# Attention scores as plain fp32 matmuls on 32 rows in place of three fp32r products

## The chip, the cores and the metric

One core of one Trainium2 chip. The time is the device time of one execution in microseconds (us). Engines in the rows: PE is TensorE's matmuls, PEld its weight loads, DVE is VectorE, ACT is ScalarE, POOL is GpSimd, SP is SyncE.

## The reference

Two cross-attention layers in fp32 over 16 batches of 128 tokens (x is 16 x 128 x 256, the context 16 x 128 x 192), 16 heads of 16:

```python
def _L0_xattn_ref(x, y, ...):
    xn = layernorm(x, ln1_w, ln1_b); yn = layernorm(y, ln2_w, ln2_b)
    q = (xn @ Wq) ...; k, v = split(yn @ Wkv)            # 16 heads of 16
    attn = softmax(einsum('bhqd,bhkd->bhqk', q, k) * scale)
    x = x + (einsum('bhqk,bhkd->bhqd', attn, v) @ Wproj + bproj)
    h = gelu(layernorm(x, ln3_w, ln3_b) @ W1 + b1, approximate=False)
    return x + (h @ W2 + b2)

def _L1_xattn_ref(x, encoder_out, norm_w, wq, wkv, wout):
    xn = x * rsqrt(mean(x * x) + EPS_RMS) * norm_w
    q = xn @ wq; k, v = split(encoder_out @ wkv)
    q = rotate(q, cos, sin); k = rotate(k, cos, sin)
    q = q / maximum(norm(q), EPS_L2); k = k / maximum(norm(k), EPS_L2)
    attn = softmax(einsum('bqhd,bkhd->bhqk', q, k) * sqrt(HEAD_DIM))
    return x + einsum('bhqk,bkhd->bqhd', attn, v) @ wout
```

## The kernel before, in words

A tile is one batch: 128 tokens, which stand in the 128 partitions. Three stages follow one another. Stage A is the attention of the first layer, stage B its MLP (two tiles at a time), stage C the second layer. x stays on the chip in x_all from the first load to the last store. Each engine has its own program, with the order of its steps written out by hand: step_a(s) and step_c(p, j) name what an engine does in step s, for tiles s, s-1, s-2 and so on, and semaphores tie the engines together.

In stage A, TensorE's step_a(s) is: queries and keys of tile s-1 (L722, L726, plain fp32, into bank_qk, already transposed: 256 query rows and 256 key rows as four blocks of 128 x 128), the turn of the finished heads of tile s-5 (L820), values of tile s-2 (L736, plain fp32), scores_a of tile s-2, the weighted values of tile s-4 (L800, plain fp32, one matmul for each of 16 heads, into four column quadrants of 32), the output projection of tile s-5 (L828), the turn of the maxima of tile s-3 (L770), the turn of the inputs of tile s (L708, L710), the turn back of tile s-4 (L811), and shifted_a of tile s-3.

scores_a gives the scores with the queries down the partitions, from which VectorE takes each row's maximum (row_max, L1203, two instructions of 128 x 1024). shifted_a computes the same scores once more, the other way round, and subtracts the maxima by further matmuls (L782, fp32r), and ScalarE takes the exponentials of these (L477). Both call score_terms, which is one score call below.

A head has 16 rows, and a quadrant of 32 partitions holds two heads. So one side of the product is in `masked`: two copies of qkT, each multiplied by a column of halves_t (ones on the 16 rows of one head of each quadrant, zeros on the other), side by side as 256 columns. One matmul on 32 rows then gives both heads. Before the change each operand is split into a high part of type fp32r and a low part (what is left, fp32r too), and the product is the sum of three fp32r matmuls, (hi, hi), (hi, lo), (lo, hi), by HI_LO. In stage A ScalarE makes the high part (queries_keys_hi, L446) and both masked copies of it (L454); VectorE makes the low part (queries_keys_lo, L1193), and GpSimd both masked copies of that (L342). A ring of RING = 3 buffers holds them.

In stage C, TensorE's step_c is: back_c, queries and keys (L697, fp32r, three products), units_T (the turn of the unit vectors, L1021, into bank_o), values_c (L697), weighted_c (L834), inputs_c (L992, L994), project_c (L697), normed_c (the turn of `on`, L1062, into bank_o as well), scores (L1032). ScalarE's units_hi writes the masked high parts of the queries and the high part of the keys from bank_o (L631 twice, L633), VectorE's units_lo the low parts (L1389 twice, L1392). normed_c waits for units_lo, because it overwrites bank_o. GpSimd takes -0.5 powers (L413, 128 x 32) for the unit vectors.

VectorE's step_a(s) is: statistics(s), heads_a(s-5), residual_a(s-6), normalise(s), queries_keys_lo(s-1), maxima(s-2); its step_c has units_lo behind turns and turned, and ahead of square_sums and inputs_lo. Each engine goes through its list strictly in order.

Of the kernel before, what the change touches and what calls it, by code (L numbers as in the profile page):

```python
# [39 lines left out]
NG = 4  # L40
# [52 lines left out]
def build(nc, x, ctx, ln1_w, ln1_b, ln2_w, ln2_b, ln3_w, ln3_b, Wq, Wkv, Wproj, bproj, W1, b1, W2, b2,  # L93
          norm_w, wq, wkv, wout, rope, halves, picks, out):
    es = ExitStack()
    with es:
# [98 lines left out]
        def att_sems(n):  # L195
# [6 lines left out]
        a_centred, a_qk_hi, a_qk_lo, a_masked_hi, a_masked_lo = (  # L202
            sem(f"a_{k}") for k in ("centred", "qk_hi", "qk_lo", "masked_hi", "masked_lo"))
# [5 lines left out]
        c_rope, c_turned, c_rot, c_rot_sq, c_norm_sq, c_norm_min, c_norm_inv, c_unit, c_unit_hi, c_unit_lo = (  # L209
            sem(f"c_{k}") for k in ("rope", "turned", "rot", "rot_sq", "norm_sq", "norm_min", "norm_inv", "unit", "unit_hi", "unit_lo"))  # L210
# [94 lines left out]
        def _(pool):  # L305
# [28 lines left out]
            def masked_lo(t):  # L334

                if ok(t):
                    r = t % RING
                    pool.wait_ge(a_qk_lo, t + 1)
                    wait(pool, a_shifted, t - 2)
                    for half in range(2):  # L340
                        ones = halves_t[:, half:half + 1].unsqueeze(2).broadcast_to([128, 4, TOK])
                        nc.gpsimd.tensor_tensor(masked[:, r, 1, :, half, :], qkT_r[:, r, 1, :, :].bitcast(fp32), ones, ALU.mult)\  # L342
                            .then_inc(a_masked_lo, 1)

            def step_a(s):
                inverse_std(s)
                residual_bias(s)
                masked_lo(s - 1)
# [7 lines left out]
            masked_lo(0)  # L356
# [3 lines left out]
            masked_lo(1)  # L360
            residual_bias(3)
            masked_lo(2)
            inverse_std(4)
            residual_bias(4)
            masked_lo(3)
# [59 lines left out]
        def _(act):  # L425
# [15 lines left out]
            def queries_keys_hi(t):  # L441

                if ok(t):
                    act.wait_ge(A["qk_mm"], t + 1)
                    wait(act, a_shifted, t - 2)
                    nc.scalar.activation(qkT_r[:, t % RING, 0, :, :], bank_qk[:, :].rearrange("p (a b) -> p a b", a=4), ACT.Copy)\  # L446
                        .then_inc(a_qk_hi, 1)

            def masked_hi(t):

                if ok(t):
                    act.wait_ge(a_qk_hi, t + 1)
                    for half in range(2):
                        nc.scalar.activation(masked[:, t % RING, 0, :, half, :], qkT_r[:, t % RING, 0, :, :].bitcast(fp32),  # L454
                                             ACT.Copy, scale=halves_t[:, half:half + 1]).then_inc(a_masked_hi, 1)
# [51 lines left out]
            def step_a(s):  # L507
                exps_a(s - 4)
                queries_keys_hi(s - 1)
                on_T(s - 5)  # L510
                masked_hi(s - 1)
# [12 lines left out]
            queries_keys_hi(0)  # L524
            inputs_T(1)
            masked_hi(0)
            values_a(0)
            queries_keys_hi(1)
            inputs_T(2)
            masked_hi(1)  # L530
            values_a(1)
            queries_keys_hi(2)
            maxima_T(0, bank_y)
            inputs_T(3)
            masked_hi(2)
            exps_a(0)
            queries_keys_hi(3)
            masked_hi(3)
# [86 lines left out]
            def units_hi(t, j):  # L625

                if ok(t):
                    act.wait_ge(c_turned, t + 1)
                    wait(act, C["scores"], NG * (t - 1))
                    for half in range(2):  # L630
                        nc.scalar.activation(pair[:, j, 0, :, half, :], bank_o[:, 0:C1].rearrange("p (a b) -> p a b", a=KT),  # L631
                                             ACT.Copy, scale=halves_t[:, half:half + 1]).then_inc(c_unit_hi, 1)
                    nc.scalar.activation(qkT_r[:, j, 0, KT:, :], bank_o[:, C1:].rearrange("p (a b) -> p a b", a=KT), ACT.Copy)\  # L633
                        .then_inc(c_unit_hi, 1)
# [25 lines left out]
            def step_c(p, j):  # L660
# [4 lines left out]
                units_hi(s - 3, 1 - j)  # L665
# [25 lines left out]
        def _(pe):  # L691
# [21 lines left out]
            def queries_keys_a(t):  # L713

                if ok(t):
                    j = t % 2
                    pe.wait_ge(A["inT_ready"], t + 1)
                    wait(pe, a_qk_lo, t)
# [771 lines left out]
```

## Time and profile before

| | us |
|---|---|
| median of 3 runs | 385.97 |
| lowest and highest | 385.35, 391.71 |
| span of the profiled execution | 386.9 |

The profiled execution has no time of its own beside its span, which runs from its first to its last instruction; it stands 0.9 us above the median of the timed runs. Stage A runs to about 150 us of the span, stage B to about 265, stage C to the end. TensorE is busy 356.5 us (92%), VectorE 294.4, ScalarE 239.3, GpSimd 197.1. A busy share is an average over the span: what bounds a stage is read from the chain of waits in that stage. TensorE's records overlap, so the sum of their lengths is more than the time that they take.

### The profile page before, as it was taken

To read this page: it belongs to the slowest core of one execution; us is meant where nothing else is said; L and a number is where in the kernel's file an instruction comes from. 1 tells how busy PE (TensorE), PEld (TensorE's weight loads), DVE (VectorE), ACT (ScalarE), POOL (GpSimd) and SP (SyncE) were. 2 spreads that over 40 slices of the span, in tenths; PEclk is the share of its full clock that TensorE was granted. 3 is DMA by queue.
4 is the path that set the end of the run, shared out by engine and by line. 5 is a ranking of instruction groups with operands and counts; after the bars stand their busy time and mean duration, and the time that the engine had idled before them with its cause. 6 is when DMAs were issued, how large, how long until landed. Compare 5 with 4: busy or idle time off the path is not lost.

```text
span 386.9 us, 11499 instructions
## 1 busy us (share of the span) xinstructions
PE 356.5 (92%) x4475; PEld 318.7 (82%) x4475; DVE 294.4 (76%) x654; ACT 239.3 (62%) x464; POOL 197.1 (51%) x177
## 2 busy tenths in 40 slices
PE   8998999999999989898999999978889989989974
PEld 5977888888888867798999998978778878878854
DVE  4799987989899773267755559467899999999752
ACT  2356677666677655815644476163877777777862
POOL 2474544554665611003331233248899998999810
PEclk9999999999999999999999999999999999999999
DMA  6853001110000000000000000000001001010001
GB/s 157 246 158 121 27 25 43 32 28 25 2 3 4 22 2 2 2 2 0 0 0 0 0 0 3 10 22 0 22 12 36 26 26 42 29 37 14 29 30 41
DMA packets 14432, 12.39 MB, mean 32 GB/s; under 512 B 2996, under 2 KB 13752, under 8 KB 14392
## 3 DMA queue, kind: packets, MB, share of 16 engines
q1 hardware_dynamic: 14384, 11.83, 10.4%
q8 instruction: 28, 0.46, 0.5%
q14 instruction: 12, 0.10, 0.1%
q10 hardware_dynamic: 8, 0.00, 0.0%
HBM read 9.73 MB, written 2.10 MB: 31 GB/s over the span
## 4 chain that ended last, share of the span: by engine, by line
PE 58%; issue 22%; DVE 10%; ACT 5%; POOL 4%; POOLq 0%; DVEq 0%; ACTq 0%
PE bank_qk L697 9%; PE banks_s L745 6%; PE bank_y L834 4%; PE bank_y L828 3%; PE banks_s L1032 3%; PE bank_t L800 3%; PE bank_qk L722 3%; PE bank_o L736 3%; PE bank_t L697 3%; PE bank_qk L726 3%; DVE row_max L1203 2%; POOL x_all L375 2%; PE bank_y L1052 2%; PE bank_o L1021 2%; PE bank_y L929 1%
## 5 line engine op out<-in xcount | busy, mean ns | idle before, releaser
L413 POOL TENSOR_TENSOR norm_inv<-norm_sq_min,minus_half 128x32 f32<-128x32 f32 x16 | 87.5, 5468 | 1.8 <-DVE norm_sq_min L1374 1.8
L576 ACT ACTIVATE W_s<-banks_s,b_cols 128x256 f32<-128x256 f32 x60 | 25.0, 469 | 41.3 <-PE banks_s L915 41.3
L342 POOL TENSOR_TENSOR masked<-qkT_r,halves_t 128x512 fp32r<-128x512 f32 x32 | 32.9, 1050 | 24.1 <-DVE qkT_r L1193 24.1
L477 ACT ACTIVATE PT<-banks_s 128x1024 f32<-128x1024 f32 x32 | 31.0, 1022 | 20.3 <-PE banks_s L782 18.3
L1203 DVE TENSOR_REDUCE row_max<-banks_s 128x8 f32<-128x1024 f32 x32 | 37.6, 1218 | 7.7 <-PE banks_s L745 7.7
L368 POOL TENSOR_TENSOR b_var_eps<-b_mean_var,eps_t 128x2 f32<-128x2 f32 x8 | 1.6, 197 | 69.1 <-DVE b_mean_var L1137 69.1
L915 PE MATMUL banks_s<-lnT_hi,W_hi 128*128 128x256 f32 x120 | 34.2, 285 | 0.0
L915 PE MATMUL banks_s<-lnT_hi,W_lo 128*128 128x256 f32 x120 | 33.9, 283 | 0.0
L915 PE MATMUL banks_s<-lnT_lo,W_hi 128*128 128x256 f32 x120 | 33.9, 283 | 0.0
L642 ACT ACTIVATE PT<-banks_s 128x1024 f32<-128x1024 f32 x32 | 31.1, 1024 | 4.1 <-PE banks_s L1032 4.1
L745 PE MATMUL banks_s<-masked,qkT_r 32*128 32x256 f32 x768 | 31.5, 294 | 1.6 <-DVE row_max L1203 1.3
L745 PEld LDWEIGHTS banks_s<-masked,qkT_r 32*128 32x128 f32 x768 | 25.0, 184 | 9.5 <-issue 7.7
L1298 DVE TENSOR_TENSOR hT_lo<-W_s,hT_hi 128x512 fp32r<-128x512 f32 x32 | 24.6, 793 | 10.2 <-ACT hT_hi L580 10.1
L375 POOL TENSOR_TENSOR x_all<-x_all,b_row 128x256 f32 (+1 forms) x16 | 15.8, 1005 | 16.0 <-DVE qk_unit L1149 16.0
L915 PEld LDWEIGHTS banks_s<-lnT_hi,W_hi 128*128 128x128 f32 x120 | 23.0, 192 | 0.2 <-issue 0.2
L915 PEld LDWEIGHTS banks_s<-lnT_lo,W_hi 128*128 128x128 f32 x120 | 23.0, 192 | 0.0
L915 PEld LDWEIGHTS banks_s<-lnT_hi,W_lo 128*128 128x128 f32 x120 | 23.0, 192 | 0.0
L454 ACT ACTIVATE masked<-qkT_r,halves_t 128x512 fp32r<-128x512 f32 x32 | 21.3, 718 | 0.0
L929 PE MATMUL bank_o<-W_hi,hT_hi 128*128 128x256 f32 x64 | 19.1, 299 | 1.5 <-DVE hT_lo L1298 1.4
L580 ACT ACTIVATE hT_hi<-W_s 128x512 fp32r<-128x512 f32 x31 | 19.6, 632 | 1.0
L319 POOL TENSOR_TENSOR var_eps<-mean_var,eps_t 128x2 f32<-128x2 f32 x16 | 3.1, 196 | 33.5 <-DVE mean_var L1168 33.5
L834 PE MATMUL bank_y<-PT,vals 128*17 128x128 f32 x512 | 17.1, 274 | 2.6 <-ACT PT L642 2.6
(171 smaller groups left out, 1095.6 us busy)
## 6 DMA issues: line engine op xcount, KB each, us to landing
ctx_in<-in_ctx SPq DMA_DIRECT2D x32, 96.0 KB, 2.0
x_all<-in_x SPq DMA_DIRECT2D x16, 128.0 KB, 2.1
W_s<-in_L_xattn_W SPq DMA_DIRECT2D x2, 1024.0 KB, 6.4
out<-Wq_s SPq DMA_DIRECT2D x16, 128.0 KB, 1.8
Wq_s<-in_L_xattn_Wq SPq DMA_DIRECT2D x1, 256.0 KB, 3.0
Wkv_s<-in_L_xattn_Wkv SPq DMA_DIRECT2D x1, 256.0 KB, 3.2
Wproj_s<-in_L_xattn_Wproj SPq DMA_DIRECT2D x1, 256.0 KB, 4.2
wout_s<-in_L_xattn_wout SPq DMA_DIRECT2D x1, 256.0 KB, 3.0
```

The lines of the kernel that those rows point to most:

```text
L342: nc.gpsimd.tensor_tensor(masked[:, r, 1, :, half, :], qkT_r[:, r, 1, :, :].bitcast(fp32), ones, ALU.mult)\
L375: nc.gpsimd.tensor_tensor(tile_of(2 * p + j), tile_of(2 * p + j), b2_row[:, :], ALU.add).then_inc(b_bias, 1)
L413: nc.gpsimd.tensor_tensor(norm_inv[:, j, :], norm_sq_min[:, j, :], minus_half[:, :], ALU.pow)\
L477: nc.scalar.activation(PT[:, 2 * h:2 * h + 2, :], banks_s[:, 2 * h:2 * h + 2, :], ACT.Exp, scale=HD ** -0.5)\
L576: last = nc.scalar.activation(hT[:, m, :], (bank or bank_s[u])[:, 256 * k:256 * k + 256], ACT.Gelu, bias=b1_cols[:, m:m + 1])
L642: nc.scalar.activation(PT[:, 2 * h:2 * h + 2, :], banks_s[:, 2 * h:2 * h + 2, :], ACT.Exp, scale=HD ** 0.5)\
L697: last = mm(out, a[:, x, k, :], b[:, y, k, :], start=k == n == 0, stop=k == 1 and n == 2)
L745: last = mm(bank_s[g][:, 2 * TOK * tile:2 * TOK * (tile + 1)], qkT_r[quad(g), r, a, rows + tile, :], masked[quad(g), r, b, columns + tile, ...
L834: last = mm(out[32 * r:32 * r + VW, 128 * g:128 * g + 128], vals[:, j, GH * g + r, :], PT[:, g, 128 * r:128 * r + 128], start=True, stop=True)
L915: last = mm((bank or bank_s[u])[:, 256 * (m % 2):256 * (m % 2) + 256], w[:, k, 128 * m:128 * m + 128], act_T[:, k, :], start=k == n == 0, ...
L1203: v.tensor_reduce(row_max[:, 8 * h:8 * h + 8], banks_s[:, 2 * h:2 * h + 2, :].rearrange("p n (r k) -> p (n r) k", k=TOK), AX.X, ALU.max).t ...
L1298: v.tensor_tensor(hT_lo[:, part(u), :], hT[:, part(u), :], hT_hi[:, part(u), :].bitcast(fp32), ALU.subtract).then_inc(b_hT_lo, 1)
```

## The change

qkT and masked become plain fp32 tiles with one part each. score_terms and stage C's scores make one plain fp32 matmul where they made three fp32r ones, so a score call is 8 matmuls and not 24. The low parts go: queries_keys_lo (VectorE, stage A) and units_lo (VectorE, stage C) are removed. In stage A ScalarE now makes the first masked copy and GpSimd the second; both wait for ScalarE's copy of bank_qk (a_qk_ready). In stage C ScalarE's three instructions stay, with plain fp32 output (units_out), and count up c_unit_T, for which TensorE now waits. All waits on a_qk_lo become waits on a_qk_ready.

```diff
-        qkT_r = sb("qkT_r", 128, RING, 2, 4, TOK, dtype=fp32r)
-        masked = sb("masked", 128, RING, 2, 4, 2, TOK, dtype=fp32r)
-        pair = masked[:, :, :, 0:KT, :, :]
+        qkT = sb("qkT", 128, RING, 4, TOK)
+        masked = sb("masked", 128, RING, 4, 2, TOK)
+        pair = masked[:, :, 0:KT, :, :]
...
-            def masked_lo(t):
+            def masked_pool(t):
...
-                    pool.wait_ge(a_qk_lo, t + 1)
+                    pool.wait_ge(a_qk_ready, t + 1)
                     wait(pool, a_shifted, t - 2)
-                    for half in range(2):
+                    for half in (1,):
                         ones = halves_t[:, half:half + 1].unsqueeze(2).broadcast_to([128, 4, TOK])
-                        nc.gpsimd.tensor_tensor(masked[:, r, 1, :, half, :], qkT_r[:, r, 1, :, :].bitcast(fp32), ones, ALU.mult)\
-                            .then_inc(a_masked_lo, 1)
+                        nc.gpsimd.tensor_tensor(masked[:, r, :, half, :], qkT[:, r, :, :], ones, ALU.mult).then_inc(a_masked_pool, 1)
...
+            def queries_keys_T(t):
...
+                    nc.scalar.activation(qkT[:, t % RING, :, :], bank_qk[:, :].rearrange("p (a b) -> p a b", a=4), ACT.Copy)\
+                        .then_inc(a_qk_ready, 1)
+
+            def masked_act(t):
+
+                if ok(t):
+                    act.wait_ge(a_qk_ready, t + 1)
+                    nc.scalar.activation(masked[:, t % RING, :, 0, :], qkT[:, t % RING, :, :], ACT.Copy, scale=halves_t[:, 0:1])\
+                        .then_inc(a_masked_act, 1)
...
                 for tile in range(KT):
-                    for n, (a, b) in enumerate(HI_LO):
-                        for g in range(QUARTERS):
-                            last = mm(bank_s[g][:, 2 * TOK * tile:2 * TOK * (tile + 1)], qkT_r[quad(g), r, a, rows + tile, :],
-                                      masked[quad(g), r, b, columns + tile, :, :], start=n == 0 and (stop or tile == 0), stop=stop and n == 2)
-                            if stop and tile == KT - 1 and n == 2:
-                                last.then_inc(A["scores"], 1)
+                    for g in range(QUARTERS):
+                        last = mm(bank_s[g][:, 2 * TOK * tile:2 * TOK * (tile + 1)], qkT[quad(g), r, rows + tile, :],
+                                  masked[quad(g), r, columns + tile, :, :], start=stop or tile == 0, stop=stop)
+                        if stop and tile == KT - 1:
+                            last.then_inc(A["scores"], 1)
...
-                    wait(pe, c_unit_lo, t)
+                    wait(pe, c_unit_T, 3 * t)
...
-                    pe.wait_ge(c_unit_lo, t + 1)
+                    pe.wait_ge(c_unit_T, 3 * t + 3)
                     wait(pe, C["exped"], 2 * t)
                     for half in range(KT):
-                        for n, (k, q) in enumerate(HI_LO):
-                            for g in range(NG):
-                                last = mm(bank_s[g][:, 2 * TOK * half:2 * TOK * (half + 1)], qkT_r[quad(g), j, k, KT + half, :],
-                                          pair[quad(g), j, q, half, :, :], start=n == 0, stop=n == 2)
-                                if half == KT - 1 and n == 2:
-                                    last.then_inc(C["scores"], 1)
+                        for g in range(NG):
+                            last = mm(bank_s[g][:, 2 * TOK * half:2 * TOK * (half + 1)], qkT[quad(g), j, KT + half, :],
+                                      pair[quad(g), j, half, :, :], start=True, stop=True)
+                            if half == KT - 1:
+                                last.then_inc(C["scores"], 1)
...
-                    pe.wait_ge(c_unit_lo, upto(t + 3))
+                    pe.wait_ge(c_unit_T, 3 * upto(t + 3))
...
-            def queries_keys_lo(t):
-
-                if ok(t):
-                    r = t % RING
-                    dve.wait_ge(a_qk_hi, t + 1)
-                    v.tensor_tensor(qkT_r[:, r, 1, :, :], bank_qk[:, :].rearrange("p (a b) -> p a b", a=4),
-                                    qkT_r[:, r, 0, :, :].bitcast(fp32), ALU.subtract).then_inc(a_qk_lo, 1)
...
-            def units_lo(t, j):
-
-                if ok(t):
-                    dve.wait_ge(c_unit_hi, 3 * t + 3)
-                    for half in range(2):
-                        v.scalar_tensor_tensor(pair[:, j, 1, :, half, :], bank_o[:, 0:C1].rearrange("p (a b) -> p a b", a=KT),
-                                               halves_t[:, half:half + 1], pair[:, j, 0, :, half, :].bitcast(fp32),
-                                               ALU.mult, ALU.subtract)
-                    v.tensor_tensor(qkT_r[:, j, 1, KT:, :], bank_o[:, C1:].rearrange("p (a b) -> p a b", a=KT),
-                                    qkT_r[:, j, 0, KT:, :].bitcast(fp32), ALU.subtract).then_inc(c_unit_lo, 1)
```

## Rows read from the trace of the kernel before

**Rows 1.** The page, part 1: busy time of each engine.

```profile
PE 356.5 (92%) x4475; PEld 318.7 (82%) x4475; DVE 294.4 (76%) x654; ACT 239.3 (62%) x464; POOL 197.1 (51%) x177
```

**Rows 2.** The view of windows; one stretch of stage A, one of C.

```profile
60.00:100.00 40.00, 40.00 (x615) 34.62 (x605) 36.15 (x84) 27.71 (x49) 19.96 (x28) 1.00 0.09 25
300.00:340.00 40.00, 36.90 (x526) 33.12 (x524) 36.97 (x84) 31.32 (x65) 36.85 (x18) 1.00 0.10 30
```

**Rows 3.** The chain of waits, one tile of stage A: start, length, what.

```profile
79.11 0.92 PE banks_s L745 x23
...
82.62 0.87 PE bank_o L736 x4
...
87.44 0.92 PE banks_s L745 x23
```

**Rows 4.** The timeline, stage A: start, length, engine, line, count, [idle before].

```profile
112.38 0.98 PE L745 MATMUL banks_s<-masked,qkT_r 32*128 32x256 f32 x24
...
115.79 1.03 PE L736 MATMUL bank_o<-Wkv_s,inT 128*128 128x256 f32 x4
...
117.21 2.04 POOL L342 TENSOR_TENSOR masked<-qkT_r,halves_t 128x512 fp32r<-128x512 f32 x2 [1.29 <-DVE qkT_r L1193]
...
117.67 1.07 PE L800 MATMUL bank_t<-PT,vals 128*17 128x128 f32 x32
```

**Rows 5.** The groups by shape, TensorE: busy in all, mean ns of one.

```profile
L745 PE MATMUL banks_s<-masked,qkT_r 32*128 32x256 f32 x768 | 31.5, 294 | 1.6 <-DVE row_max L1203 1.3 <-ACT PT L477 0.2
...
L800 PE MATMUL bank_t<-PT,vals 128*17 128x128 f32 x512 | 17.1, 274 | 0.6 <-ACT maxT L469 0.6
...
L736 PE MATMUL bank_o<-Wkv_s,inT 128*128 128x256 f32 x64 | 16.5, 380 | 0.0
```

**Rows 6.** The timeline, start of the kernel: one row against 512 columns.

```profile
4.72 2.07 PE L868 MATMUL bank_qk<-PT,vals 1*128 1x512 f32 x2
```

**Rows 7.** The timeline, first tiles of stage A.

```profile
20.36 0.98 PE L745 MATMUL banks_s<-masked,qkT_r 32*128 32x256 f32 x24
...
21.29 0.66 DVE L1193 TENSOR_TENSOR qkT_r<-bank_qk,qkT_r 128x512 fp32r<-128x512 f32 x1
...
21.86 2.35 DVE L1203 TENSOR_REDUCE row_max<-banks_s 128x8 f32<-128x1024 f32 x2
...
26.53 0.68 DVE L1193 TENSOR_TENSOR qkT_r<-bank_qk,qkT_r 128x512 fp32r<-128x512 f32 x1
...
27.13 2.34 DVE L1203 TENSOR_REDUCE row_max<-banks_s 128x8 f32<-128x1024 f32 x2
```

**Rows 8.** The chain of waits, one tile of stage C.

```profile
311.10 0.39 ACT vals L623
...
312.26 0.72 PE bank_qk L697 x6
...
313.20 0.91 PE banks_s L1032 x22
...
320.44 0.92 PE banks_s L1032 x21
```

**Rows 9.** The timeline, one tile of stage C: VectorE and GpSimd.

```profile
310.80 0.87 DVE L1389 SCALAR_TENSOR_TENSOR masked<-bank_o,halves_t,masked 128x256 fp32r<-128x256 f32 x2
...
311.58 0.41 DVE L1392 TENSOR_TENSOR qkT_r<-bank_o,qkT_r 128x256 fp32r<-128x256 f32 x1
...
315.19 5.44 POOL L413 TENSOR_TENSOR norm_inv<-norm_sq_min,minus_half 128x32 f32<-128x32 f32 x1
```

**Rows 10.** The timeline, first tile of stage C: TensorE.

```profile
270.48 0.99 PE L1032 MATMUL banks_s<-masked,qkT_r 32*128 32x256 f32 x24 [0.50 <-DVE qkT_r L1392]
...
271.89 0.98 PE L697 MATMUL bank_qk<-wq_r,inT_r 128*128 128x256 f32 x6 [0.42 <-DVE inT_r L1348]
```

**Rows 11.** The timeline, last tile but one of stage C.

```profile
373.98 0.41 DVE L1392 TENSOR_TENSOR qkT_r<-bank_o,qkT_r 128x256 fp32r<-128x256 f32 x1
...
374.50 0.41 PE L1062 MATMUL bank_o<-ident,on 128*128 128x128 f32 x2 [0.27 <-issue]
```

More of the change, by code:

```diff
@@ L201, in build @@
         A, C = att_sems("a"), att_sems("c")
-        a_centred, a_qk_hi, a_qk_lo, a_masked_hi, a_masked_lo = (
-            sem(f"a_{k}") for k in ("centred", "qk_hi", "qk_lo", "masked_hi", "masked_lo"))
+        a_centred, a_qk_ready, a_masked_act, a_masked_pool = (
+            sem(f"a_{k}") for k in ("centred", "qk_ready", "masked_act", "masked_pool"))
         a_maxed, a_max_hi, a_max_lo, a_max_turned, a_maxT, a_shifted = (
@@ L355, in _ @@
             inverse_std(2)
-            masked_lo(0)
+            masked_pool(0)
             residual_bias(1)
@@ L523, in _ @@
             nc.scalar.activation(picks_wide[:, :, :], each(picks_t[:, :], GH, TOK), ACT.Copy).then_inc(picks_ready, 1)
-            queries_keys_hi(0)
+            queries_keys_T(0)
             inputs_T(1)
-            masked_hi(0)
+            masked_act(0)
             values_a(0)
-            queries_keys_hi(1)
+            queries_keys_T(1)
             inputs_T(2)
-            masked_hi(1)
+            masked_act(1)
             values_a(1)
-            queries_keys_hi(2)
+            queries_keys_T(2)
             maxima_T(0, bank_y)
             inputs_T(3)
-            masked_hi(2)
+            masked_act(2)
             exps_a(0)
-            queries_keys_hi(3)
-            masked_hi(3)
+            queries_keys_T(3)
+            masked_act(3)
             out_T(0)
@@ L630, in units_hi @@
                     for half in range(2):
[L631 to L634, printed above, removed]
+                        nc.scalar.activation(pair[:, j, :, half, :], bank_o[:, 0:C1].rearrange("p (a b) -> p a b", a=KT),
+                                             ACT.Copy, scale=halves_t[:, half:half + 1]).then_inc(c_unit_T, 1)
+                    nc.scalar.activation(qkT[:, j, KT:, :], bank_o[:, C1:].rearrange("p (a b) -> p a b", a=KT), ACT.Copy)\
+                        .then_inc(c_unit_T, 1)
             def exps(t):
@@ L717, in queries_keys_a @@
                     pe.wait_ge(A["inT_ready"], t + 1)
-                    wait(pe, a_qk_lo, t)
+                    wait(pe, a_qk_ready, t)
                     wait(pe, a_maxT, t - 2)
@@ L1236, in step_a @@
                 norm(s)
-                queries_keys_lo(s - 1)
                 maxima(s - 2)
@@ L1246, in _ @@
             statistics(2)
-            queries_keys_lo(0)
             normalise(2)
             statistics(3)
-            queries_keys_lo(1)
             maxima(0)
             normalise(3)
-            queries_keys_lo(2)
             maxima(1)
@@ L1256, in _ @@
             normalise(4)
-            queries_keys_lo(3)
             maxima(2)
@@ L1428, in step_c @@
                 turned(s - 1, 1 - j)
-                units_lo(s - 3, 1 - j)
                 square_sums(s - 1, 1 - j)
```

36 lines of the change are left out of this document (14 added, 22 removed).

## The prediction

> **What bounds the kernel now.** I read the page first: TensorE is busy 92% of the span, more than any other engine, but VectorE has 76% and the average says nothing of single stages [rows 1]. The view of windows by stage comes next. In the middle of stage A TensorE is busy for 40.00 of 40 us and VectorE for 36.15; in stage C TensorE, VectorE and GpSimd all stand near 36.9 of 40; the granted clock is 1.00, its upper level of 2.4 GHz, in both [rows 2]. So in A one engine is full and the next has 10% to spare, and in C three are close together. Which wait ends last is then read from the chain of waits. In A it never leaves TensorE: one tile takes 87.44 - 79.11 = 8.33 us, and the pieces are matmuls back to back [rows 3]. In C one tile takes 320.44 - 313.20 = 7.24 us; the chain is TensorE but for one hop per tile, to ScalarE's copy of the values (0.39 us) and back [rows 8]. VectorE's and GpSimd's long instructions, GpSimd's 5.44 us power among them, are not in it. Both attention stages are therefore set by the time that TensorE needs, and work taken from VectorE, ScalarE or GpSimd is worth something only in the filling and draining of the stages. Stage B between them is not touched.
>
> **The price of a score call on TensorE.** A score call is now 24 matmuls of 32 rows against 256 columns. They go to four row quadrants, so four run side by side: six turns. On the chain a call takes 0.92 us [rows 3, 8]. A full-height fp32r matmul of the same 256 columns takes 0.72 / 6 = 0.12 us of the chain [rows 8]; six turns are 0.72, and 0.20 us is left for the two ends of a call (first weights, change of the array's division). After the change a call is 8 plain fp32 matmuls. The trace shows each plain fp32 matmul as two records: stage A's values are 2 matmuls and 4 records, L800 is 16 matmuls and 32 [rows 4]. So a call becomes 16 records in four turns. A plain fp32 record of 256 columns takes 0.87 / 4 = 0.216 us [rows 3]. Four turns are 0.86, with the same ends 1.07 us: **+0.15 us a call**.
>
> The bounds of this price. Above: a record that costs two fp32r passes, 4 x 0.24 + 0.20 = 1.16, or +0.24. The L800 records give a value between: 32 of them in 1.07 us, the last taking 0.27, are seven steps of 0.114 for 128 columns, 0.228 for 256, and +0.19 a call [rows 4, 5]. Below: a record on 32 rows that streamed like an fp32r one would give 4 x 0.12 + 0.20 = 0.68, or -0.24. No row supports this: the one fp32 product on few rows, a single row against 512 columns, took over 1 us a record, so fewer rows made nothing shorter [rows 6]. I take +0.15, since L736 is the same type and width.
>
> The Trainium skill, "FP8 and Floating Point Precision", section TensorE Precision Notes, speaks against the change: true fp32 is four passes through the array, where three fp32r products are three. By it a call's streaming grows from six passes to eight, which would be +0.24 us. The trace agrees in sign and puts the size lower, as a plain record takes 0.216 us and not 0.24 [rows 3, 8].
>
> **That four still run side by side** is what the whole sum hangs on, as no row shows plain fp32 on row quadrants. Two near rows do each half: fp32r on row quadrants is four wide (24 records of 0.12 us each would be 2.9 us one after another, and take 0.98), and plain fp32 on column quadrants is four wide (32 records of 0.11 would be 3.5 us, and take 1.07) [rows 4]. In L800, too, the two records of a matmul aim at one quadrant and the next matmul at another, and 32 records still need only eight turns. I take it to hold.
>
> **Where the price falls.** Stage A has 32 calls (scores_a and shifted_a of 16 tiles), C has 16. Five of A's fall before 40 us, where VectorE leads; they are dealt with below. The other 27 and the 16 of C lie in stretches where the chain runs through TensorE: 43 x 0.15 = **+6.5 us**. A tile of A goes from 8.33 to 8.63 us, a tile of C from 7.24 to 7.39.
>
> **What is taken from the other engines.** In A: from VectorE queries_keys_lo, 0.68 us a tile; from GpSimd one of two masked copies, half of 2.04 us [rows 4, 7]; from ScalarE one of two. In C: from VectorE units_lo, 0.87 + 0.41 us a tile [rows 9]; ScalarE's three instructions stay. GpSimd's copy now waits for ScalarE's qkT instead of VectorE's low part, which comes later, and TensorE waits in C for ScalarE's third copy instead of VectorE's: no wait is added, each is moved earlier. Behind TensorE's wait stand the scores, and behind these VectorE's maxima or ScalarE's exponentials. In full swing all of this is worth nothing, for TensorE covers it. If that cover were gone, 0.68 us a tile would come off A and 1.28 off C.
>
> It pays in four places. (1) The filling of A: VectorE goes in order, and row_max of tile 0 and 1 start when the copies of 0.66 and 0.68 us ahead of them are over. Without the first, row_max waits for the scores, which end at 20.36 + 0.98 + 0.15 = 21.49 instead of 21.86: 0.4 us. Without the second it is 0.6 more (27.13 - 26.53) [rows 7]. Two of the longer calls lie behind on the way to 40 us: -1.0 + 0.3 = **-0.7 us**. (2) The first tile of C: TensorE waits 0.50 us for VectorE's low part and 0.42 for inT_r queued behind it [rows 10]. The first wait goes; the second is then ScalarE's inT_r copy and VectorE's after it: **-0.5**. (3) The draining of C: TensorE's turn of `on` waits until units_lo of the last tiles is over; it starts at 374.50, some 0.1 us after the copy of 0.41 us that starts at 373.98, and had sat idle for 0.27 [rows 11]. Three such steps, **-0.7**. (4) Around 120 us VectorE has stage B's first normalisation too; I leave its few tenths out. Together -1.9.
>
> **Sum.** +6.5 - 1.9 = +4.6 us. The profiled execution has a span of 386.9 us; by the sum it becomes 391.5. The span stands 0.9 above the median of the timed runs, 385.97, so the forecast for these is **390.5 us**, 1.2% slower. With +0.19 a call it is 392.2, with +0.24 it is 394.4.
>
> **Rivals.** (a) The two records of one matmul hold each other up. If TensorE started matmuls strictly in order, the second record of a matmul would wait for the first, which has its quadrant, and only neighbours would overlap: nine turns for eight matmuls instead of four, (9 - 4) x 0.216 = +1.08 more a call, with +0.15 it is 1.23, and over 48 calls +59 - 2: **443 us**, slower. It decides as soon as the order of start is fixed; L800's 32 records would then need 17 turns of 0.11, 1.9 us, and show 1.07 [rows 4]. The Trainium skill, "TensorE: Matmul & The Clock Gate", Part 3, says that matmuls start and end strictly in program order, which by itself would give this case; the 1.07 us of L800 does not agree. (b) Plain fp32 on row quadrants isn't side by side at all: 16 x 0.216 + 0.20 = 3.66 us, +2.74 a call, 48 calls +131: about **515 us**. For it speaks only that no row shows the combination. (c) The streaming costs nothing more (a record near 0.18 us, or ends that overlap better), and VectorE's relief alone is left: 385.97 - 1.9 = **384 us**. VectorE at 36 of 40 us speaks for relief being felt, the chain without a VectorE piece against it [rows 2, 3]. (d) A record on 32 rows streams as fast as an fp32r one: -0.24 x 43 - 1.9, **374 us**; rows 6 speak against it.
>
> **How the numbers follow.** The forecast's case, four wide at +0.12 to +0.24 a call, has 0.76; (a) 0.07, (b) 0.04, (c) 0.10, (d) 0.03. The forecast's case alone spans 388.5 to 394.5, and 1.5 more if a longer last record (0.38 against 0.29 us) [rows 5] is felt by VectorE and ScalarE behind it. The range takes in (c) and this and leaves (a), (b), (d) out: 384 to 396. A measurement of this kernel tells about 2% from no change, 7.7 us. Slower by more than that are (a), (b) and the upper edge of the forecast's case, 0.11 + 0.10; faster (d) and a little, 0.04; the rest, 0.75, is within.
>
> **What would show it.** Score calls on the chain at 1.07 us instead of 0.92, each with 16 records of some 0.38 us, four starting together; tiles of A at 8.6 us and of C at 7.4; VectorE in A near 79% busy instead of 90 (8.33 x 0.90 - 0.68 = 6.8 of 8.63 us), with the chain still on TensorE; the scores of tile 0 of C no longer waiting for VectorE. The forecast is wrong if a call takes 2 us or more (a, b), or if the tile of A does not lengthen (c): then either a plain record is cheaper on 32 rows, or VectorE held TensorE up in a way that the chain does not show.

## The result and the profile after

The changed kernel takes 393.26 us (median of 4 runs, 393.04 to 395.39). The kernel before, run beside it, takes 387.32 us (median of 4, 385.35 to 391.71). The ratio is 1.0192 with a 95% interval of 1.0141 to 1.0244: slower by 1.9%, at the edge of what this measurement calls a difference of 2%. The prediction was 390.5 us with a range of 384 to 396.

One thing is needed to read the spans below: the executions of every kernel here fall into groups, by whether the first microseconds took some 3 to 4 us longer (a late start) and by whether the granted clock fell on the way (a mean of 0.994 to 0.996 instead of 1.0); one with neither is called undisturbed. The kernel before then has a span of 383.6 to 384.3 us, 384.0 below. Its profiled execution of 386.9 us had a late start. The changed kernel's profiled execution has 390.5 us, started without delay, and had one fall of the clock.

The pace of TensorE shows what a late start is. TensorE's program begins with transposes of the identity, all alike. Windows of 2 us, two of the kernel before and one of the changed kernel:

```profile
8.00:10.00 2.00, 2.00 (x11) 2.00 (x11) 0.88 (x3) 0.98 (x2) 0.00 (x0) 1.00 0.72 91
11.00:13.00 2.00, 2.00 (x20) 2.00 (x19) 1.69 (x6) 0.06 (x1) 1.37 (x3) 1.00 1.02 404
```

```profile
8.00:10.00 2.00, 2.00 (x21) 2.00 (x20) 1.96 (x8) 0.12 (x1) 0.17 (x1) 1.00 0.91 79
```

In the kernel before, a transpose starts every 0.213 us up to 10.8 us of the span and every 0.109 us from there on; in the changed kernel the step comes at 4.4 us. The trace has records of the granted clock only from 10.81 us on in the one and from 4.38 us on in the other, and the view writes 1.00 where it has none. So that TensorE ran at the lower of its two levels (1.2 GHz) until then is inferred, from half the pace for the same instruction. The other profiled executions agree: the first record stands at 13.2 to 13.6 us in the three with a late start (experiments 3 to 5) and at 4.4 to 5.5 us in the rest.

The page of the changed kernel, engines, answers to [rows 1]:

```profile
PE 362.1 (93%) x4091; PEld 318.4 (82%) x4091; DVE 268.7 (69%) x590; ACT 229.2 (59%) x448; POOL 181.1 (46%) x161
```

TensorE has 384 records fewer (48 calls, 24 down to 16) and yet is busy 5.6 us longer. All other engines have less to do. The view of windows, same stretches as [rows 2]:

```profile
60.00:100.00 40.00, 40.00 (x526) 33.80 (x528) 32.94 (x77) 24.69 (x42) 16.12 (x24) 1.00 0.09 25
300.00:340.00 40.00, 36.90 (x463) 31.85 (x462) 31.35 (x66) 30.76 (x67) 35.04 (x18) 1.00 0.12 35
```

VectorE in stage A fell from 36.15 to 32.94 of 40 us (82%), in C from 36.97 to 31.35. TensorE stayed where it was, full in A. The chain of waits of a tile of stage A answers to [rows 3]:

```profile
73.62 1.08 PE banks_s L742 x16
...
81.40 0.87 PE bank_o L734 x4
82.27 1.08 PE banks_s L742 x16
```

From 73.62 to 82.27 is one tile: 8.65 us, 8.33 before, still without a piece of another engine. Each of its two score calls (the other is at 77.74) takes 1.07 or 1.08 us instead of 0.92. L734, which the change does not touch, has its 0.87 as before. The chain of a tile of stage C, to [rows 8]:

```profile
301.30 1.08 PE banks_s L1028 x16
...
306.62 0.39 ACT vals L621
...
307.77 0.72 PE bank_qk L695 x6
...
308.71 1.07 PE banks_s L1028 x16
```

308.71 - 301.30 = 7.41 us, 7.24 before, with the same hop to ScalarE. The groups by shape and the timeline, to [rows 5] and [rows 4]:

```profile
L742 PE MATMUL banks_s<-masked,qkT 32*128 32x256 f32 x512 | 36.7, 400 | 1.2 <-DVE row_max L1191 0.7 <-ACT PT L475 0.3
```

```profile
77.67 1.15 PE L742 MATMUL banks_s<-masked,qkT 32*128 32x256 f32 x16
```

At the pace of L734, 0.216 us a record, sixteen one after another would need 3.5 us; the call takes 1.07 on the chain. In the trace the records start four at a time, within some 0.02 us, and the last three fours 0.216 us apart. So four run side by side, as the prediction took it.

I divided both traces at the first TensorE instruction of a step (turns of the inputs, of `on`, stage B, stage C, the turn of unit vectors of a given tile). The lengths are worked out from the start times, not rows of a view; microseconds, one profiled execution of each kernel, from TensorE's first matmul to the end of VectorE's last instruction:

```
stretch                                before  changed  difference
first matmul to first turn of inputs    10.70     7.64   -3.06
stage A filling                         28.27    28.52   +0.25
stage A body                            96.27    99.70   +3.43
stage A draining (two steps of B in it) 20.87    21.49   +0.62
stage B                                 87.69    87.65   -0.04
seam of B and C                         21.82    23.34   +1.52
stage C filling                         19.66    19.43   -0.23
stage C body                            78.46    80.11   +1.65
stage C draining                        19.40    18.87   -0.53
```

The differences sum to +3.6, that of the two spans (390.5 - 386.9). Three things are in it: the price of the score calls, +3.43 and +1.65 in the two bodies; where stages fill and drain, small losses in A (+0.25, +0.62) and small gains in C (-0.23, -0.53); and 1.52 us at the seam of B and C, which the prediction did not have. The start is the late start named above.

The windows of 2 us at the seam show what the 1.52 us are, first in the changed kernel, then in the kernel before (the third number from the end is the granted clock):

```profile
258.00:260.00 2.00, 0.77 (x7) 0.80 (x8) 1.49 (x4) 1.94 (x6) 1.79 (x2) 1.00 0.00 0
260.00:262.00 2.00, 2.00 (x13) 2.00 (x13) 1.34 (x3) 0.97 (x2) 2.00 (x1) 0.60 0.23 56
262.00:264.00 2.00, 2.00 (x12) 2.00 (x12) 1.94 (x3) 0.00 (x0) 2.00 (x1) 0.55 0.01 2
```

```profile
257.00:259.00 2.00, 0.96 (x9) 0.99 (x10) 1.29 (x4) 1.97 (x5) 1.78 (x2) 1.00 0.00 0
259.00:261.00 2.00, 2.00 (x20) 2.00 (x19) 1.68 (x3) 0.78 (x2) 2.00 (x1) 1.00 0.24 57
```

The granted clock is 0.60 and 0.55 in two windows of 2 us: some 3.4 of the 4 us at the lower of its two levels (1.2 GHz), and TensorE gets through 13 and 12 records where the kernel before gets through 20. The timeline of TensorE there, changed kernel:

```profile
259.24 0.41 PE L989 MATMUL bank_t<-ident,xn 128*128 128x128 f32 x2 [2.30 <-ACT vals L621]
...
260.43 1.48 PE L695 MATMUL bank_qk<-wkv_r,inT_r 128*128 128x256 f32 x6
```

L695's six records take 1.48 us instead of 0.88. What the engine did before is an idle time of 2.30 us, waiting for ScalarE's copy of the values. The kernel before has the same idle time, 2.30 us at 258.04, and in its profile the clock stays at 1.00. The runs beside this profile tell that it is no single mishap: three of the changed kernel's four have a span of 390.5 or 390.6 and a mean clock of 0.995.

Time outside the span is a last difference: 2.3 to 2.8 us in the changed kernel's four runs, 1.7 to 1.8 in all 17 of the kernel before in the first set.

### The profile page after: what moved, and what is told of

Read it like the earlier page. It is cut to its first block, busy times and chain, and to the rows that moved or that the text cites. A ratio compares the mean times of both kernels' runs of the same rounds, so it can differ in the third digit from the quotient of the medians.

```text
span 390.5 us, 10645 instructions
## 1 busy us (share of the span) xinstructions
PE 362.1 (93%) x4091; PEld 318.4 (82%) x4091; DVE 268.7 (69%) x590; ACT 229.2 (59%) x448; POOL 181.1 (46%) x161
## 4 chain that ended last, share of the span: by engine, by line
PE 62%; issue 21%; DVE 7%; ACT 5%; POOL 4%; POOLq 0%; DVEq 0%; ACTq 0%
PE bank_qk L695 9%; PE banks_s L742 8%; PE bank_y L831 4%; PE banks_s L1028 4%; PE bank_t L797 4%; PE bank_qk L720 4%; PE bank_y L825 4%; PE bank_qk L724 3%; PE bank_o L734 3%; PE bank_t L695 3%; POOL x_all L374 2%; PE bank_y L1048 2%; PE bank_o L1018 2%; DVE row_max L1191 1%; PE bank_y L926 1%
## 5 line engine op out<-in xcount | busy, mean ns | idle before, releaser
L742 PE MATMUL banks_s<-masked,qkT 32*128 32x256 f32 x512 | 36.7, 400 | 1.2 <-DVE row_max L1191 0.7
L742 PEld LDWEIGHTS banks_s<-masked,qkT 32*128 32x128 f32 x512 | 23.2, 184 | 9.7 <-issue 7.8
L342 POOL TENSOR_TENSOR masked<-qkT,halves_t 128x512 f32<-128x512 f32 x16 | 17.4, 1089 | 13.7 <-ACT qkT L445 13.7
L483 ACT ACTIVATE oT<-bank_t 128x512 f32<-128x512 f32 x16 | 9.5, 596 | 21.8 <-PE bank_t L797 21.8
L1355 DVE TENSOR_REDUCE norm_sq<-rot_sq 128x32 f32<-128x512 f32 x16 | 11.0, 685 | 16.3 <-ACT rot_sq L614 16.3
```

Of the source, the lines that this page charges most:

```text
L742: last = mm(bank_s[g][:, 2 * TOK * tile:2 * TOK * (tile + 1)], qkT[quad(g), r, rows + tile, :], masked[quad(g), r, columns + tile, :, :], ...
```

## The experiments

Theory 1 held that TensorE's calls are dearer by 0.15 us each and that this is the loss, reduced a little by the relief of VectorE, and that the rest is the fall of the clock. The rivals gave the relief more weight, or made the order of start matter, or put the clock down to chance. Experiments 1 to 4 shared 17 runs of the kernel before, 5 to 8 another 17, and 9 another 17. Each ratio is to the runs of its own set.

**Experiment 1, the price alone.** The kernel before, with its low parts still made by VectorE, GpSimd and ScalarE, and one plain fp32 product in each score call:

```diff
-                    for n, (a, b) in enumerate(HI_LO):
-                        for g in range(QUARTERS):
-                            last = mm(..., qkT_r[quad(g), r, a, rows + tile, :],
-                                      masked[quad(g), r, b, columns + tile, :, :], ...)
+                    for g in range(QUARTERS):
+                        last = mm(..., qkT_r[quad(g), r, 0, rows + tile, :].bitcast(fp32),
+                                  masked[quad(g), r, 0, columns + tile, :, :].bitcast(fp32), ...)
```

and the same in stage C.

> The kernel before with one edit: each score call makes one plain fp32 product of the high parts instead of three fp32r products. VectorE still makes the low parts and GpSimd still masks them, and nobody reads them, so the output lacks the low parts' share of the scores. Theory 1 (TensorE's price is the whole of it, the relief of the other engines is worth next to nothing): 43 calls on the chain x 0.155 = +6.5 to +7.5 us, some 393 us, and a tile of stage A at 8.65 us. Rival (the price is larger, +9 us or more, because the longer last record also delays VectorE and ScalarE, and the relief gives 2 to 3 us of it back in the changed kernel): 396 us or more.

Measured: 396.78 us (median of 6, 393.39 to 397.97), ratio 1.0222 (1.0154 to 1.0289). Its chain of waits in A, and its window of 60 to 100 us:

```profile
73.80 1.08 PE banks_s L744 x16
...
82.46 1.08 PE banks_s L744 x16
```

```profile
60.00:100.00 40.00, 40.00 (x524) 33.81 (x526) 34.69 (x83) 26.99 (x47) 19.07 (x27) 1.00 0.09 25
```

One tile is 8.66 us, as in the changed kernel, though VectorE has nearly all of its old work per tile (34.69 of 40 us, with fewer tiles in the stretch). The one undisturbed run has 390.9 us, 6.9 above the 384.0 of the kernel before. The price alone is larger than the whole loss.

**Experiment 2, the relief alone.** The changed kernel with fp32r tiles and its one product made three times, so that a score call has 24 records again while nothing of the removed copies comes back:

```diff
-        qkT = sb("qkT", 128, RING, 4, TOK)
-        masked = sb("masked", 128, RING, 4, 2, TOK)
+        qkT = sb("qkT", 128, RING, 4, TOK, dtype=fp32r)
+        masked = sb("masked", 128, RING, 4, 2, TOK, dtype=fp32r)
...
-                    for g in range(QUARTERS):
+                    for n in range(3):
+                        for g in range(QUARTERS):
```

> The changed kernel with one edit: qkT and masked are fp32r tiles and each score call makes the same fp32r product three times, so TensorE does what it did before and the other engines do what they do after. The scores come out three times too large. Theory 1: between 0 and -1 us against the kernel before, a tile of stage A at 8.33 us, although VectorE has 0.68 us less to do in it. Rival: -2 to -3 us (the sum of the prediction, -1.9), or more if VectorE held TensorE up in ways that the chain doesn't show.

Measured: 386.02 us (median of 12, 384.08 to 389.81), ratio 0.9984 (0.9936 to 1.0032). The profiled run is undisturbed:

```profile
67.58 0.92 PE banks_s L743 x23
...
75.92 0.92 PE banks_s L743 x23
```

The tile is 8.34 us, 8.33 before: in full swing the relief buys nothing. The undisturbed spans, 382.3 and 382.4 us, are 1.65 below 384.0, between what theory and rival had said. Divided as above, it is -0.24 in A's filling, -0.15 in A's body, -0.27 in C's filling, -0.88 in C's draining. The two halves add up: +6.9 - 1.65 = +5.25, and the changed kernel without its clock fall (experiment 5) is at +5.0.

**Experiment 3, the order of start.** The changed kernel, both matmuls of a row quadrant one after the other:

```diff
-                for tile in range(KT):
-                    for g in range(QUARTERS):
+                for g in range(QUARTERS):
+                    for tile in range(KT):
```

> The changed kernel with the two inner loops of a score call swapped: both matmuls of a quadrant, four records, follow one another before the next quadrant's turn. Theory 1 (TensorE starts records of other quadrants past a waiting one): 1.07 to 1.08 us a call as in the changed kernel, the same time within 1 us. Rival (starts follow program order strictly): 13 turns of 0.216 us instead of 4, +1.9 us a call, 48 calls, some 480 us. Between them (a window that is short): a call of 1.2 to 1.6 us, 5 to 25 us more.

Measured: 396.25 us (median of 6), ratio 1.0194 (1.0132 to 1.0257). The timeline:

```profile
78.20 1.17 PE L742 MATMUL banks_s<-masked,qkT 32*128 32x256 f32 x16
```

Four records in a row now aim at one quadrant. If TensorE started them strictly in order, only the last of one quadrant and the first of the next would overlap: 13 turns of 0.216, some 3.0 us a call. It takes 1.17 us by the timeline against 1.15, and 1.08 to 1.10 on the chain. Records of other quadrants start past one that waits for its own. The order isn't quite free: the two runs of this kernel with a quick start have spans of 391.7 and 391.8 us, 1.2 above the changed kernel's 390.5, with the clock's fall in both kernels, as 48 calls some 0.02 us longer would give.

**Experiment 4, the idle time at the seam filled.** The changed kernel with 28 transposes of the identity, into a bank free at that time, in the idle time:

```diff
+            pe.wait_ge(b_x, 2 * NP - 2)
+            busy(28)
```

> The changed kernel with 28 transposes of the identity into bank_y while TensorE waits for ScalarE's Gelus at the seam of stages B and C; the output is untouched. In the changed kernel's profile the granted clock fell to 0.55 to 0.60 for the 4 us after that wait, and the chain there was 1.5 us longer than before. Theory 1 (the clock fell because TensorE stood idle there): the clock stays 1.00 and the time falls by 1 to 2 us. Rival (the fall has nothing to do with the idle stretch, or the transposes delay the matmuls behind them): the same time or up to 1 us more.

Measured: 393.18 us (median of 6, 391.36 to 395.86), ratio 1.0131 (1.0064 to 1.0197). Timeline and windows of its seam (this run's start was slow, so the seam comes later):

```profile
261.22 3.22 PE L858 MATMUL bank_y<-ident 128*128 128x128 f32 x28
264.28 0.38 PE L989 MATMUL bank_t<-ident,xn 128*128 128x128 f32 x2
```

```profile
264.00:266.00 2.00, 2.00 (x20) 2.00 (x18) 1.05 (x2) 1.48 (x3) 2.00 (x1) 1.00 0.04 10
```

The clock stays at 1.00, and four of the six runs have a mean clock of 1.0. But 28 transposes last longer than the idle time of 2.30 us, and L989 waits for them: the seam takes 22.40 us, where it took 21.82 before the change. The fastest runs are 389.5 to 389.9.

**Experiment 5, the same with 20 transposes.** Only the number differs.

> The changed kernel with 20 transposes at the seam of stages B and C instead of 28: TensorE's wait there was 2.3 us in the changed kernel's profile, and a transpose takes 0.11. With 28 the clock held in all runs that had it at the start, but the seam was 0.57 us longer than in an undisturbed run. Theory 1 (the idle stretch lets the clock fall): granted clock 1.00 across the seam, and the seam no longer than undisturbed, so undisturbed spans of 389.0 us, 0.6 less than with 28 and 1.5 less than with the fall. Rival (fewer transposes don't hold the clock): the fall comes back, 390.5.

Measured: 395.13 us (median of 6, 390.89 to 395.96), ratio 1.013 (1.0057 to 1.0203), four of the six with a late start. The timeline of the seam:

```profile
260.99 2.34 PE L858 MATMUL bank_y<-ident 128*128 128x128 f32 x20
263.44 0.41 PE L989 MATMUL bank_t<-ident,xn 128*128 128x128 f32 x2
```

The transposes are over when L989's data come, the seam takes 21.83 us, none of the six runs has a mean clock below 0.997 (three of the changed kernel's four have), and the two runs without a late start have spans of 389.0 and 389.1 us at a clock of 1.0. Against the changed kernel's 390.5 the fall was worth 1.5 us; against 384.0 the change itself costs 5.0.

**Experiment 6, one fp32r product where only the maximum is wanted.** If TensorE's passes are what is paid, the cheap place for them is scores_a, whose result only gives the maximum that is subtracted. The kernel before, with scores_a on the high parts alone; the exact scores are still three products:

```diff
-                    for n, (a, b) in enumerate(HI_LO):
+                    for n, (a, b) in enumerate(HI_LO[:1] if stop else HI_LO):
```

> The kernel before with one edit: scores_a, which serves only the row maxima, makes one fp32r product of the high parts (8 matmuls instead of 24). The maxima are then rounded, and the shift that the softmax cancels is a little off; the scores that are exponentiated keep all three products. Theory 1 (TensorE's time is the time in stage A): 4 turns of 0.12 us less for each of 16 tiles, a tile of A at 7.85 us, and 6 to 7.5 us less in all, 379 us. Rival (VectorE, with 7.5 us of work a tile, becomes the bound at once, or the loop of scores, maxima, shift and exponentials does): a tile of A at 8.0 to 8.2 us and 2 to 5 us less.

Measured: 382.84 us (median of 12, 382.43 to 386.95), ratio 0.9898 (0.9852 to 0.9943). The chain and the window:

```profile
73.88 0.91 PE banks_s L745 x23
...
78.26 0.44 PE banks_s L745 x7
...
81.74 0.91 PE banks_s L745 x24
```

```profile
60.00:100.00 40.00, 40.00 (x584) 34.39 (x583) 38.00 (x88) 29.61 (x52) 22.41 (x31) 1.00 0.09 25
```

A tile is 7.86 us, 0.47 less, from one call that went from 0.92 to 0.44. VectorE reaches 38.00 of 40 us, and in these tiles it is not yet in the chain. From 94.5 us on it is; the chain's next pieces, and one of the tile after:

```profile
95.68 1.23 DVE row_max L1203
...
105.38 1.11 DVE max_cols L1209
```

So the rival is right about the later tiles, of which the next three take 8.47, 7.86 and 9.53 us from one row_max to the next, and the gain is not 16 x 0.47 = 7.5 us: without the clock's fall it is 4.9 (experiment 9). L1209, a copy of 16 columns that takes 0.17 us elsewhere, takes 1.11 here; GpSimd's split of stage B's weights runs beside it. All twelve runs have a mean clock of 0.994 to 0.996, and in the profiled one the fall begins at 250.56 us, behind the same wait of the seam (2.29 us, ended at 250.43): it comes in this kernel too, which has none of the change's edits.

**Experiments 7 and 8, VectorE without TensorE's cover.** One fp32r product in all score calls, in 7 on experiment 2's kernel (low copies not made), in 8 on the kernel before (low copies made, not read). Experiment 7's edit, with the same in stage C:

```diff
-                    for n in range(3):
+                    for n in range(1):
```

Experiment 8 has `HI_LO[:1]` in both loops.

> Both stages with one fp32r product in each score call, and no low parts made by VectorE (the other engines as in the changed kernel). The low parts' share of the scores is left out. If TensorE alone set the time, 43 calls x 0.48 = -20.6 us and the relief's -1.6: 364 us, tiles of A at 7.37 us and of C at 6.76. If other loops come up first: more than that, at most 6 us.

> The kernel before with one fp32r product in each score call; VectorE still makes the low parts, which nobody reads. The low parts' share of the scores is left out. TensorE has the same work as in the run with one product and no low parts. Theory 1 (relief of VectorE is worth something once TensorE no longer covers it): a tile of A is held by VectorE at about 7.6 to 8.0 us, and the run is 6 to 12 us slower than the one without low parts. Rival (VectorE isn't near to being the bound even then): 1.6 us between the two, as with three products.

Measured: 7 has 373.63 us (median of 4), ratio 0.9636 (0.9552 to 0.972); 8 has 375.19 us, ratio 0.9702 (0.9611 to 0.9793). Windows of 7 and of 8, then the chain of 7 and of 8, then a timeline row of each:

```profile
60.00:100.00 40.00, 39.42 (x538) 32.80 (x535) 39.02 (x85) 26.71 (x47) 20.49 (x29) 1.00 0.09 25
```

```profile
60.00:100.00 40.00, 38.48 (x505) 31.99 (x503) 39.09 (x90) 30.36 (x53) 23.20 (x33) 1.00 0.09 25
```

```profile
68.58 2.35 DVE row_max L1193 x2
...
75.75 2.35 DVE row_max L1193 x2
```

```profile
69.59 2.35 DVE row_max L1203 x2
...
76.78 2.35 DVE row_max L1203 x2
```

```profile
67.46 1.19 DVE L1183 SCALAR_TENSOR_TENSOR yn<-yn,rstd,ln_rows 128x192 f32<-128x192 f32 x1
```

```profile
68.66 0.41 DVE L1185 SCALAR_TENSOR_TENSOR yn<-yn,rstd,ln_rows 128x192 f32<-128x192 f32 x1
```

In both, the chain of A has here gone over to VectorE: TensorE's cover is gone, as it never was in the changed kernel. Yet the copy of 0.68 us a tile is worth little even now: one tile takes 7.17 us in 7 and 7.19 in 8 by these rows (the next, in which VectorE also splits a part of stage B's weights, 8.19 and 8.25), A's whole body 87.83 against 89.91, the profiled spans 370.0 against 372.2. That is nearer the rival's 1.6 us than the theory's 6 and more, though the rival's reason, that VectorE is far from being the bound, is not what the chains show. In 7's profile the clock also falls a second time, at 360.1 us; if that cost what the fall at the seam cost, the spans are some 3.7 us apart without it, an estimate.

VectorE is busy for as long with less to do (39.02 and 39.09 of 40 us), and the traces show with what. Its second step on yn is the same instruction in both. It takes 1.19 us in 7, beside GpSimd's masked copy, and 0.41 in 8, where that copy comes later and no GpSimd instruction lies beside it. From 36 to 124 us the mean of eleven is 1.06 us in 7 and 0.41 in 8: of the 0.68 us taken away, 0.65 a tile came back there.

**Experiment 9, both edits that helped.** Experiment 6 with the 20 transposes of experiment 5 at the seam.

> The kernel before with both edits that helped: the maxima from one fp32r product, and 20 transposes at the seam of stages B and C, where the clock fell in all 12 runs of the kernel with the first edit alone. Theory 1 (the fall costs 1.5 us and the transposes stop it): granted clock 1.00 across the seam, spans of 379.2 us where the start is quick, against 380.7 with the first edit alone and 384.0 for the kernel before, so 381 us and 3 to 7 us less than before. Rival (the seam's matmuls are pushed back by the transposes as much as the clock gives): 380.7 us spans.

Measured: 384.51 us (median of 12, 380.95 to 385.62), ratio 0.9912 (0.987 to 0.9954). The profiled run is undisturbed, 379.1 us at a clock of 1.000, 4.9 below the kernel before and 1.5 below experiment 6's quick starts (380.6 to 381.1, all with the fall); four runs are 380.5 to 381.1 with a mean clock of 0.995, so the fall was not held off in these, or came elsewhere. The others started late. By the medians experiment 6 and 9 gain about 0.9%, without the change under study. The transposes add nothing that these 12 runs can separate.

## Why the prediction was nearly right, and where it was not

**The price of a call.** Predicted 1.07 us from four turns of 0.216 and the old ends of 0.20; measured 1.07 and 1.08, in both stages and in experiment 1. Tiles: 8.65 against 8.63 in A, 7.41 against 7.39 in C. Taking the price from the plain fp32 row of the same width [rows 3] was the step that carried the forecast. The two records of one matmul do not hold each other up, rival (a) is out, and (b), (c) and (d) with it. The Trainium skill, "TensorE: Matmul & The Clock Gate", Part 3, has matmuls start and end strictly in program order; experiment 3's 1.17 us with four records in a row on one quadrant doesn't agree, at least for the start. The Trainium skill's four passes for true fp32 ("FP8 and Floating Point Precision", TensorE Precision Notes), each at the 0.12 us of an fp32r matmul, would have given +0.24 us a call, an estimate, where +0.15 was measured.

**How many calls pay.** Predicted 43 and +6.5 us; the price alone costs 6.9 by the undisturbed run, some 45 calls of 0.155. The body of A, 23 calls, has +3.43: 23 x 0.155 less the 0.15 of relief that experiment 2 has there. The prediction's lower edge for this case, 388.5, doesn't follow from its own terms: 385.97 + 43 x 0.12 - 1.9 is 389.2.

**[Rows 6] as a bound.** The same two instructions take 1.12 us in the changed kernel:

```profile
4.59 1.12 PE L865 MATMUL bank_qk<-PT,vals 1*128 1x512 f32 x2
```

So the 2.07 us of rows 6 was no price: it lies in the first 10.8 us of that run, where TensorE kept half its pace, while in the changed kernel the pair begins behind the step at 4.4 us. The 1.00 of the view had no record behind it there. The conclusion drawn from the row stands, since some 0.48 us a record of 512 columns (4.59 to 5.55, where the next begins) is 0.24 for 256; "over 1 us a record" does not, and the row should have been read against a second one.

**The relief.** Predicted -1.9 in three places, measured -1.65 in experiment 2, otherwise spread. C's first tile is right in its waits: the one of 0.50 us [rows 10] is gone, and the next one is inT_r's, as said. Over C's whole filling only 0.27 of the 0.5 us is left.

```profile
272.63 1.15 PE L1028 MATMUL banks_s<-masked,qkT 32*128 32x256 f32 x16
274.27 0.98 PE L695 MATMUL bank_qk<-wq_r,inT_r 128*128 128x256 f32 x6 [0.49 <-DVE inT_r L1331]
```

C's draining gave -0.88 instead of -0.7; the turn of `on` no longer waits [rows 11]. The chain of the changed kernel has it at once behind the projection, 0.22 us long:

```profile
377.20 0.91 PE bank_qk L695 x6
378.11 0.22 PE bank_o L1058 x2
378.32 1.20 PE banks_s L1028 x16
```

A's filling failed: -0.24 instead of the -1.0 ahead of the longer calls. The step that failed is "Without the second it is 0.6 more". The timelines of VectorE and of GpSimd in the changed kernel, then VectorE's row of the kernel before:

```profile
22.89 1.19 DVE L1181 SCALAR_TENSOR_TENSOR yn<-yn,rstd,ln_rows 128x192 f32<-128x192 f32 x1
24.01 2.34 DVE L1191 TENSOR_REDUCE row_max<-banks_s 128x8 f32<-128x1024 f32 x2
```

```profile
22.65 1.22 POOL L342 TENSOR_TENSOR masked<-qkT,halves_t 128x512 f32<-128x512 f32 x1
```

```profile
26.20 0.40 DVE L1185 SCALAR_TENSOR_TENSOR yn<-yn,rstd,ln_rows 128x192 f32<-128x192 f32 x1
```

GpSimd's copy no longer waits for VectorE's low part, so it comes earlier, and lies beside VectorE's second step on yn. That step takes 1.19 us instead of 0.40, and is over 0.2 us after GpSimd's copy is. The 0.68 us of the removed copy are eaten by the 0.79 that its neighbour grew. The prediction did move GpSimd's copy earlier, and asked only who waits for it, not what it would run beside. The Trainium skill, "GPSIMD Engine Reference", Specifications, says that GpSimd's SBUF interfaces are shared with VectorE, with contention where the VectorE instruction has two SBUF inputs, as this one has; these rows agree, and it is the rule that should have been weighed.

**The clock at the seam.** The prediction had nothing for it: it listed no case in which the granted clock changes, and read 1.00 in both stages as given [rows 2]. It is 1.5 of the 2.8 us by which 390.5 was too low. Experiments 4 and 5 show that it is the clock, and that filling the idle time ahead of it holds it. Why the mean clock is 0.995 in three of the changed kernel's four runs and 0.994 to 0.996 in all twelve of experiment 6, and below 0.996 in only 15 of 51 of the kernel before, with the same 2.30 us of idle time at the seam, is not settled. The runs add two things. Fourteen of those 15 have spans of 389.2 to 390.0 us, as long as a late start (387.8) and a fall (1.5) together, and none of the kernel's spans of 383.6 to 384.3 has it. And in the five profiles that have the fall (the changed kernel, experiments 1, 6, 7 and 8) it begins 0.1 to 1.3 us behind that wait.

**From the sum to the time.** The forecast took the 0.9 us between span and median as an offset. It was none: the profiled run before had a late start, and time outside the span was 1.8 us. The undisturbed 384.0, +5.0 and 1.8 give 390.8, so that this error happened to cost nothing. The account of 393.26 is 384.0 + 5.0 + 1.5 + some 2.6 outside the span, together 393.1. The 0.7 us more outside the span, against the kernel before, are unexplained; experiments 4 and 5, which are the changed kernel and some transposes, have 1.8 to 1.9 again, experiment 1 has 1.9 to 3.0 and experiment 3 1.7 to 2.7.

**VectorE's share** came out at 82% in A, not 79: 32.94 / 40 x 8.65 = 7.1 us a tile instead of 6.8. Experiment 2, with 33.73 of 40 us and a tile of 8.34, has 7.0. The groups of VectorE from 36 to 124 us, kernel before and changed kernel, show where most of it came back:

```profile
L1185 DVE SCALAR_TENSOR_TENSOR yn<-yn,rstd,ln_rows 128x192 f32<-128x192 f32 x10 | 4.1, 406 | 0.0
```

```profile
L1181 DVE SCALAR_TENSOR_TENSOR yn<-yn,rstd,ln_rows 128x192 f32<-128x192 f32 x10 | 6.5, 646 | 0.0
```

It is the step on yn again, 0.24 us a tile on average: three of the ten take 1.19 to 1.22 us, and these lie beside GpSimd's masked copy. In full swing it costs the changed kernel nothing, since TensorE covers it; in experiment 7 it costs nearly all that the removed copy would have given.

## What to carry to other kernels

Where TensorE leads, count its turns: one plain fp32 product on 32-row quadrants costs four turns of 0.216 us, three fp32r products six of 0.12, so removing two thirds of the instructions still makes the call longer, and the work taken off the other engines only pays while stages fill and drain. Before moving a GpSimd instruction earlier, look up which VectorE instruction it will then run beside. Where a term of a sum comes from a row of the first microseconds, or a span is compared with a median, check first that the execution is an undisturbed one, by the pace of equal instructions and not by the view's clock alone.

## What the runs showed of the hardware that was not expected

- The four row quadrants run plain fp32 side by side in both orders of the matmuls that were tried: sixteen records in 1.15 us, and 1.17 with the quadrants one after another.
- A VectorE instruction of two tensor inputs went from 0.40 to 1.19 us beside one GpSimd tensor_tensor, and GpSimd's from 1.04 to 1.22. VectorE's copy of 16 columns went from 0.17 to 1.11 us beside another.
- After 2.30 us without a matmul the granted clock was 0.60 and 0.55 over the next two windows of 2 us in the changed kernel, which cost 1.5 us; after the same idle time it was 1.00 in the profile of the kernel before. With 20 or 28 transposes in the gap it was 1.00 in the profiles.
- With the same instructions at the start, TensorE kept half its pace (a transpose every 0.213 us, then every 0.109) up to 10.8 us in the profile of the kernel before and up to 4.4 us in that of the changed kernel, which made the start 3.06 us longer. The view's granted clock shows 1.00 throughout, without a record behind it up to these times.
